# Low parts of three integer weights on GpSimd in place of VectorE, with new order tables for head and tail

## The reference

```python
xn = _layernorm(x, axis=-1)
s = _L0_attn_ref(xn, Wq, Wk, Wv, Wo)          # causal softmax attention, 16 heads of 16
g = _silu(_L0_ffn_ref(xn, w_gate, w_up, w_down))   # 256 -> 768 -> 256, weights int32 in -127..127, times 1/127
x = x + s * g
```

## Time and profile before

| | us |
|---|---|
| runs shown | 977.41, 979.42, 975.25; median 977.41 |
| profiled execution | 978.36, its span 976.6 |
| TensorE busy | 933.3 (96% of the span) |
| VectorE, ACT, GpSimd busy | 702.8, 579.5, 496.9 |

### The profile page before, as it was taken

The page is one execution under the profiler, slowest core; times in us unless marked ns, Lnnn a source line. Parts: engine busy times, 40 slices in busy tenths (PEclk is TensorE's granted clock), DMA queues, the critical chain, the costliest instruction groups (busy, mean ns, idle before and its releaser), DMA issues.

```text
span 976.6 us, 22669 instructions
## 1 busy us (share of the span) xinstructions
PE 933.3 (96%) x9034; PEld 690.7 (71%) x9034; DVE 702.8 (72%) x946; ACT 579.5 (59%) x793; POOL 496.9 (51%) x673
## 2 busy tenths in 40 slices
PE   5679999999999999999999999999999999999995
...
GB/s 259 161 68 99 133 84 141 147 132 158 122 173 96 195 126 131 158 121 171 100 183 137 132 158 122 170 99 195 126 132 157 122 173 99 192 126 132 113 101 83
DMA packets 86059, 135.01 MB, mean 138 GB/s; under 512 B 13504, under 2 KB 36288, under 8 KB 85952
## 3 DMA queue, kind: packets, MB, share of 16 engines
...
## 4 chain that ended last, share of the span: by engine, by line
PE 79%; issue 5%; DVE 4%; DMA 4%; ACT 3%; POOL 3%; SPq 1%; POOLq 0%; ACTq 0%; DVEq 0%
PE bank L191 42%; PE values L521 12%; PE bank L426 12%; PE bank L488 8%; PE bank L439 5%; ACT probs L496 2%; POOL o_compact L562 2%; DVE gated L371 1%; ACT o_hi L569 1%; SPq L314 1%; DMA o_reciprocals<-scratch_r 1%; DVE row_max L451 1%; DMA scratch_r<-sum_reciprocals 1%; PE bank L457 1%; DMA mean_and_rstd<-scratch_m 1%
## 5 line engine op out<-in xcount | busy, mean ns | idle before, releaser
L451 DVE TENSOR_REDUCE row_max<-bank 128x2 f32<-128x768 f32 (+3 forms) x352 | 384.6, 1124 | 70.2 <-PE bank L439 65.8
L496 ACT ACTIVATE probs<-bank 128x1024 f32<-128x1024 f32 x320 | 320.1, 1025 | 125.1 <-PE bank L488 125.0
L503 POOL TENSOR_SCALAR_AFFINE_SELECT probs<-probs 128x256 f32<-128x256 f32 (+1 forms) x448 | 195.3, 453 | 288.9 <-ACT probs L496 286.5
L426 PE MATMUL bank<-k_stack,q_stack 64*128 64x128 f32 (+3 forms) x1024 | 160.3, 372 | 10.7 <-DMA q_stack<-qk_hi 5.1
L521 PE MATMUL values<-probs,v 128*17 128x512 f32 (+3 forms) x2048 | 166.4, 436 | 1.8 <-POOL probs L503 1.6
L385 POOL TENSOR_TENSOR h_lo<-gated,h_hi 128x512 fp32r<-128x512 f32 x96 | 124.1, 1294 | 55.7 <-ACT h_hi L382 53.5
L488 PE MATMUL bank<-q_stack,k_stack 64*128 64x512 f32 (+3 forms) x1024 | 142.7, 351 | 6.0 <-issue 5.0
L426 PEld LDWEIGHTS bank<-k_stack,q_stack 64*128 64x128 f32 x1024 | 86.2, 189 | 79.4 <-issue 37.3
L488 PEld LDWEIGHTS bank<-q_stack,k_stack 64*128 64x128 f32 x1024 | 83.2, 186 | 46.7 <-issue 23.4
L358 DVE SCALAR_TENSOR_TENSOR gated<-gated,bank 128x512 f32<-128x512 f32 x96 | 65.7, 686 | 51.5 <-ACT gated L355 51.5
L439 PE MATMUL bank<-causal_mask,half_identities_bf 64*128 64x128 bf16 (+3 forms) x1408 | 100.4, 228 | 0.0
...
## 6 DMA issues: line engine op xcount, KB each, us to landing
...
x_in<-x SPq DMA_DIRECT2D x16, 512.0 KB, 3.7
...
x_again<-x SPq DMA_DIRECT2D x16, 512.0 KB, 4.6
...
```

What stands on the lines that cost most here:

```text
L426: nc.tensor.matmul(PS[:, n, j * keys:(j + 1) * keys], r(QS[par][low:low + STACK, pair, i * P:(i + 1) * P]), r(KS[par][low:low + STACK, pai ...
L451: signal(e.tensor_reduce(rows, scores, axis=AX.X, op=ALU.max), "d_sm")
L496: signal(e.activation(PR[:, (SCORES * beta + k) % SLOTS, :, :], both(banks), ACT.Exp, scale=SCALE_S), "d_ex")
L503: last = e.affine_select(out=diag, in_=diag, compare_op=ALU.is_ge, fill=0.0, base=0, pattern=[[0, many], [1, P]], channel_multiplier=-1)
```

## The change

GpSimd gets a new unit, `wi k`, that subtracts the high part of the k-th integer weight, with a semaphore of its own; VectorE keeps the subtraction for q, k, v and o alone. Users of g, u and d wait for the new semaphore. The cast and the high part stay in `wt`.

```diff
         def weights_split(e, beta, w):
 
             if beta == 0:
-                wait(e, c_wl, ORDER.index(w) + 1)
+                wait(e, *((c_wi, "gud".index(w) + 1) if w in "gud" else (c_wl, "kqvo".index(w) + 1)))
...
-            elif en == "dve":
-                if src.dtype == FP32:
-                    e.wait_ge(s_w[w], 16)
+            elif en == "dve" and src.dtype == FP32:
+                e.wait_ge(s_w[w], 16)
                 e.wait_ge(c_wh, k + 1)
                 e.tensor_tensor(r(W[w][1][:]).rearrange("p t n -> p (t n)"), stage,
                                 W[w][0][:].rearrange("p t n -> p (t n)"), ALU.subtract).then_inc(c_wl, 1)
...
+        def u_wi(en, e, beta, par, k, banks, prev):
+            w, src, stage = WEIGHTS[(2, 3, 6)[k]]
+            if en == "pool":
+                e.wait_ge(c_wf, k + 1)
+                e.wait_ge(c_wh, (2, 3, 6)[k] + 1)
+                e.tensor_tensor(r(W[w][1][:]).rearrange("p t n -> p (t n)"), stage,
+                                W[w][0][:].rearrange("p t n -> p (t n)"), ALU.subtract).then_inc(c_wi, 1)
...
             if en == "dve" and k == 0:
-                e.wait_ge(c_wl, len(W))
+                e.wait_ge(c_wi, 3)
```

`HEAD` and `TAIL` are new as a whole; `PERIOD` is as before. The beginning of `HEAD`, before and after:

```diff
-    ld 1 0, la 0 0, lb 0 0, wt 0 0, tr 0 0 6, tr 0 1 1, wt 0 1, wt 0 2, qk 0 0 6, wt 0 3, qk 0 1 2, wt 0 4, gg 0 0 1, wt 0 5,
-    ls 0 0, gg 0 1 5, gu 0 0 6, ls 0 1, wt 0 6, qk 0 2 2, qk 0 3 5, sm 0 0 34, mk 0 0 34, ls 0 2, sm 0 1 01, mk 0 1 01,
-    gu 0 1 6, la 1 0, hs 0 0, sm 0 2 56, xr 0 0, mk 0 2 56, sm 0 3 23, mk 0 3 23, gg 0 2 4, lm 1 0, v 0 0 1, sm 0 4 56,
...
+    la 0 0, lb 0 0, wt 0 0, ld 1 0, wt 0 1, tr 0 0 0, tr 0 1 1, wt 0 2, wt 0 3, wt 0 4, qk 0 0 6, wi 0 0, lt 1 0, qk 0 1 3,
+    la 1 0, v 0 0 6, wi 0 1, qk 0 2 0, ls 0 0, gg 0 0 6, gg 0 1 2, wt 0 5, gg 0 2 1, qk 0 3 6, gu 0 0 2, sm 0 0 01,
+    mk 0 0 01, wt 0 6, ls 0 1, sm 0 1 56, wi 0 2, lb 1 0, mk 0 1 56, sm 0 2 34, mk 0 2 34, gu 0 1 0, sm 0 3 56, mk 0 3 56,
...
```

In `TAIL` the scores come somewhat earlier, `mt 1 1` now stands ahead of `or 0 1` (before: behind it), `gg 1 3` went from behind `dn 1 0` to behind `st 1 12`, and `gu 1 3` from behind `st 1 12` to behind `gg 1 5`. A part of it, not aligned line by line:

```diff
-    sm 1 20 56, mk 1 20 56, pv 1 2, hs 1 2, sm 1 21 01, mk 1 21 01, st 1 7 45, or 0 1, pv 1 3, mt 1 1 6, st 1 8 01,
-    st 1 9 23, dn 1 0 4, gg 1 3 2, ob 0 1, st 1 10 56, pv 1 4, on 0 1, pv 1 5, st 1 11 34, od 1 0, os 0 1, st 1 12 01,
...
+    hs 1 2, pv 1 1, sm 1 21 34, od 0 1, mk 1 21 34, pv 1 2, st 1 7 01, mt 1 1 4, st 1 8 56, st 1 9 23, or 0 1, dn 1 0 0,
+    pv 1 3, st 1 10 34, ob 0 1, st 1 11 56, pv 1 4, pv 1 5, on 0 1, st 1 12 12, gg 1 3 5, os 0 1, st 1 13 23, st 1 14 01,
```

More of the change, by code:

```diff
@@ L54 @@
 HEAD = table("""
-    ld 1 0, la 0 0, lb 0 0, wt 0 0, tr 0 0 6, tr 0 1 1, wt 0 1, wt 0 2, qk 0 0 6, wt 0 3, qk 0 1 2, wt 0 4, gg 0 0 1, wt 0 5,
-    ls 0 0, gg 0 1 5, gu 0 0 6, ls 0 1, wt 0 6, qk 0 2 2, qk 0 3 5, sm 0 0 34, mk 0 0 34, ls 0 2, sm 0 1 01, mk 0 1 01,
-    gu 0 1 6, la 1 0, hs 0 0, sm 0 2 56, xr 0 0, mk 0 2 56, sm 0 3 23, mk 0 3 23, gg 0 2 4, lm 1 0, v 0 0 1, sm 0 4 56,
-    mk 0 4 56, sm 0 5 23, mk 0 5 23, sm 0 6 01, sm 0 7 56, mk 0 6 01, mk 0 7 56, sm 0 8 34, sm 0 9 01, mk 0 8 34, mk 0 9 01,
@@ new lines @@
+    la 1 0, v 0 0 6, wi 0 1, qk 0 2 0, ls 0 0, gg 0 0 6, gg 0 1 2, wt 0 5, gg 0 2 1, qk 0 3 6, gu 0 0 2, sm 0 0 01,
+    mk 0 0 01, wt 0 6, ls 0 1, sm 0 1 56, wi 0 2, lb 1 0, mk 0 1 56, sm 0 2 34, mk 0 2 34, gu 0 1 0, sm 0 3 56, mk 0 3 56,
+    sm 0 4 34, sm 0 5 12, mk 0 4 34, mk 0 5 12, sm 0 6 56, mk 0 6 56, sm 0 7 34, hs 0 0, sm 0 8 12, mk 0 7 34, hs 0 1,
+    mk 0 8 12, sm 0 9 45, mk 0 9 45, lm 1 0, sm 0 10 01, mk 0 10 01, ls 0 2, v 0 1 6, lc 1 0, fl 0 0, sm 0 11 12, ls 0 3,
+    mk 0 11 12, gu 0 2 0, mt 0 0 5, gg 0 3 6, sm 0 12 12, mk 0 12 12, sm 0 13 45, ld 2 0, mk 0 13 45, sm 0 14 23, mk 0 14 23,
@@ new lines @@
+    sm 0 15 01, mk 0 15 01, gg 0 4 6, st 0 0 23, st 0 1 45, hs 0 2, sm 0 16 01, fl 0 1, mk 0 16 01, if 0 0, st 0 2 23,
+    st 0 3 56, pv 0 0, la 2 0, sm 0 17 12, mk 0 17 12, st 0 4 34, gu 0 3 0, st 0 5 56, sm 0 18 34, mk 0 18 34, pv 0 1,
+    gg 0 5 1, gu 0 4 0, lx 1 0, gu 0 5 4, pv 0 2, st 0 6 56, sm 0 19 23, mk 0 19 23, dn 0 0 1, hs 0 3, qk 1 0 4, sm 0 20 23,
+    lm 2 0, ls 1 0, st 0 7 56, mk 0 20 23, pv 0 3, sm 0 21 01, st 0 8 45, mk 0 21 01, qk 1 1 6, gg 1 0 4, hs 0 4, ls 1 1,
+    mt 0 1 1, gu 1 0 3, gg 1 1 6, v 1 0 4, qk 1 2 3, gu 1 1 5, qk 1 3 0, st 0 9 12, sm 1 0 34, sm 1 1 56, mk 1 0 34,
@@ new lines @@
+    mk 1 1 56, st 0 10 12, pv 0 4, hs 0 5, pv 0 5, st 0 11 01, sm 1 2 34, ls 1 2, mk 1 2 34, lt 2 0, sm 1 3 56, mk 1 3 56,
+    gg 1 2 2, sm 1 4 34, mk 1 4 34, od 0 0, st 0 12 01, st 0 13 56, ls 1 3, st 0 14 01, sm 1 5 34, lc 2 0, mk 1 5 34, pv 0 6,
+    sm 1 6 56, mk 1 6 56, st 0 15 34, sm 1 7 01, mk 1 7 01, gu 1 2 2, sm 1 8 34, sm 1 9 56, or 0 0, ob 0 0, mk 1 8 34,
+    mk 1 9 56, dn 0 1 1, sm 1 10 23, st 0 16 56, mk 1 10 23, v 1 1 0, sm 1 11 45, hs 1 0, mk 1 11 45, mt 1 0 2, pv 0 7,
+    hs 1 1, st 0 17 01, on 0 0, sm 1 12 45, st 0 18 23, mk 1 12 45, pv 0 8, gg 1 3 0, sm 1 13 12, st 0 19 34, mk 1 13 12,
@@ new lines @@
+    pv 0 9, hs 1 2, st 1 0 56, pv 0 10, sm 1 14 23, mk 1 14 23, st 1 1 56, sm 1 15 01, mk 1 15 01, gu 1 3 4, pv 0 11,
+    sm 1 16 01, lb 2 0, st 1 2 23, mk 1 16 01, os 0 0, gg 1 4 4, dn 1 0 5, st 1 3 12, gu 1 4 4, sm 1 17 56, mk 1 17 56,
+    sm 1 18 23, od 0 1, zr 0 0, st 1 4 01, mk 1 18 23, gg 1 5 4, gu 1 5 6, sm 1 19 01, sm 1 20 23, lx 2 0, mk 1 19 01,
+    st 1 5 45, xr 0 0, mk 1 20 23, pv 1 0, hs 1 3, hs 1 4, pv 1 1, qk 2 0 6, pv 1 2, sm 1 21 45, ls 2 0, mk 1 21 45,
+    st 1 6 01, qk 2 1 2, mt 1 1 5, v 2 0 0, ls 2 1, gg 2 0 4, or 0 1, st 1 7 56, st 1 8 01, hs 1 5, qk 2 2 3, pv 1 3,
@@ new lines @@
+    st 1 9 45, st 1 10 12, qk 2 3 0, st 1 11 45, pv 1 4, sm 2 0 23, mk 2 0 23, sm 2 1 01, ob 0 1, st 1 12 56, mk 2 1 01,
+    on 0 1, pv 1 5, gu 2 0 4, st 1 13 23, od 1 0, ls 2 2, sm 2 2 01, mk 2 2 01, sm 2 3 56, pv 1 6, mk 2 3 56, sm 2 4 01,
+    mk 2 4 01, st 1 14 23, pv 1 7, sm 2 5 56, os 0 1, sm 2 6 12, sm 2 7 34, ls 2 3, mk 2 5 56, mk 2 6 12, mk 2 7 34,
+    dn 1 1 0, hs 2 0, op 0 0 5, sm 2 8 12, or 1 0, st 1 15 34, mk 2 8 12, gg 2 1 6, op 0 1 0, sm 2 9 34, st 1 16 56,
+    mk 2 9 34, sm 2 10 12, pv 1 8, mk 2 10 12, st 1 17 56, gu 2 1 0, mt 2 0 1, gg 2 2 4, sm 2 11 23, hs 2 1, mk 2 11 23,
@@ L84 @@
+    sm 2 12 56, st 1 18 01, mk 2 12 56, v 2 1 4, st 1 19 01, xr 1 0, sm 2 13 23, mk 2 13 23, sm 2 14 56, mk 2 14 56, pv 1 9,
+    sm 2 15 01, st 2 0 34, mk 2 15 01, pv 1 10""")
 PERIOD = table("""
```

14 lines of the change are left out of this document (7 added, 7 removed).

## The result

| | before | after |
|---|---|---|
| median of the runs beside each other, us (7 each) | 976.83 | 982.15 |
| profiled execution, us | 978.36 | 982.43 |
| its span, us | 976.6 | 980.6 |

The ratio is 1.0063, 95% interval 1.0044 to 1.0081: 5.3 us slower by the medians and 6.1 by the ratio, where +2.6 was forecast. The time lies inside the range given (975.0 to 984.5). By the ratio it lies just outside "within 0.5%", on the side to which the prediction leaned.

What follows compares the result with a forecast made beforehand. The time TensorE leaves the flag's branch was taken as the head's cost, with the middle saturated by TensorE. Head +2.3, afterwards -0.5, tail +0.8 gave +2.6 on the median 977.4: 980.0 us, range 975.0 to 984.5.

Steps and rivals of the forecast that it cites:

- Subtractions worth nothing by themselves: Head: VectorE loses 5.84 us ahead of its bound stretch, gaining nothing; GpSimd takes 3.8 us for each subtraction.
- x_in at 27.7, k stack at 31.2, u_lo at 34.5: Head landings and end, in us; the earlier x_transposed load delays the k stack by 1.5, from 29.74.
- The order on ACT: Head: third qk copy ahead of the gates' tanh; `qk 0 3` starts at 33.1, TensorE idles 6.6 us, before 5.1.
- First maximum at 38.95: Head: VectorE's first row maximum starts at 38.95 us, against 33.52 before.
- VectorE's stretch to the flag, 25.2 us: Head, first maximum to flag: 24.5 us after removing earlier work, plus 0.7 added; flag at 64.2 against 61.92.
- -0.5 afterwards: After the branch: TensorE's 0.5 us wait for xt_lo should go, -0.5 us (0 to -1.0).
- The tail, +0.8: Tail: maxima writes issued before the reciprocals make `od 1 0` 0.8 us later (0 to 1.5).
- Nothing else: Other reorderings in and behind the head: nothing, -0.5 to +0.5 us; no new TensorE waits between branch and PERIOD.
- +2.3: Head: TensorE returns from the branch at 69.1 us, 2.3 us late (bounds 0.8 to 3.9).
- (a): Rival, head: VectorE's work counts as a whole, 5.84 us come off the flag, 971.6 us; chance 0.10.
- (b): Rival, head and tail: load hidden, k stack at 29.7, tail 0; 977.7 us; chance 0.15.
- (c): Rival, head: GpSimd is the gate, TensorE waits for u_lo ending after 35.8; 981.8 to 983.1 us; chance 0.20.

Runs made afterwards that it cites:

- engine_alone: The kernel before, in its own order, with only the three subtractions moved from VectorE to GpSimd; ratio to before 1.0014.
- gates_first: The changed kernel with batch 1's power and the third qk copy moved behind gates 0 to 2 on ACT; ratio to before 1.0023.
- changed_again: The changed kernel itself, unaltered, run a second time; ratio to before 1.0060.
- values_early: The changed kernel with the second half of v moved to the gap before the scores, on a free bank; ratio to before 1.0050.
- tail_alone: The kernel before with only the new tail table; ratio to before 1.0028.
- tables_alone: The kernel before with both new order tables, VectorE still doing all the subtractions; ratio to before 1.0091.

## Why the prediction was right where it was, and wrong where it was not

The sign and the main mechanism were right; the size was less than half of what came. By its own steps:

- **Subtractions worth nothing by themselves.** Right: engine_alone. Each took 3.5 us, not 3.8, so the estimate from h_lo's 1.29 was high by 9%. Longer operations of GpSimd do not quite hold that rate: the 128x1024 one on x_transposed took 2.42 us in the kernel before, not 2.58. The 3.3 us estimated from the Trainium skill's GPSIMD Engine Reference, section Elementwise, was nearer. The advice of that page of the Trainium skill, VectorE for elementwise work, made no difference that engine_alone could show (1.0014, 0.9994 to 1.0034).
- **x_in at 27.7, k stack at 31.2, u_lo at 34.5.** 27.97, 31.32, 34.50 in the first profile; the others have 26.6 to 26.8 and 30.0 to 30.2. The load's 1.5 us is 1.4.
- **The order on ACT.** Right as the wait that ended last, and in the main term: `qk 0 3` starts at 33.38 (33.1), the gap is 6.7 us (6.6), the clock behind it 0.50. gates_first gives most of it back, but moves the waits for x_in and u_lo with it, so ACT's own share is read, not shown.
- **First maximum at 38.95.** 39.76, 38.66 and 37.48; mean 38.6. The sum has a slip: from 33.1 its own rows, 2.94 and 2.62 us, give 36.0 and 38.7 for the ends of `qk 0 3` and `gu 0 0`, not 35.8 and 38.0. Measured were 36.08 and 38.72 in the first profile, whose maximum came at 39.76. That the mean lies so near 38.95 is in part luck.
- **VectorE's stretch to the flag, 25.2 us.** This is the term that was mis-sized: 26.65, 26.6 and 26.3, so 1.3 us more. I took out old work and counted 0.7 us for what came in. VectorE's work was as counted (24.6 us of the 26.65); what was too small is its waiting, 1.8 to 2.1 us for gates. Both orders have the same four units on TensorE beside the reductions, but before, gate 3 was the third, with v behind it, and the granted clock was back at 1.00 when it began; in the new order v comes first and gate 3 is the fourth, at 0.50 (the windows above) when it begins. The rows, of before and then of after:

```profile
53.68 0.39 PE L191 MATMUL bank<-xt_hi,wg_hi 128*128 128x256 f32 x1
```

```profile
57.98 0.56 PE L191 MATMUL bank<-xt_hi,wg_hi 128*128 128x256 f32 x1
```

  In changed_again the wait fell one gate later (1.81 us), where the granted clock was 0.50 again. values_early took 0.9 of the waits away, and the stretch was 0.8 shorter. The prediction had called TensorE half fed beside VectorE; the earlier trace rows has it busy for 16.93 of 20 us, so there was little room.
- **Flag to return, 4.9 us.** 4.7, 5.1, 4.9.
- **-0.5 afterwards.** Not seen. The wait for xt_lo is gone as said, but from the return to the fifth reciprocal the three take 160.9, 161.3 and 161.6 us, and the three with the old head (before, engine_alone, tail_alone) 161.1, 161.5 and 161.2. The windows behind the branch, of before and then of after, name a candidate: the clock is full from about 70.6 in before, 3.7 us after the return, and from about 76.1 in after, 5.0 us after it. A matmul of 256 columns takes 0.21 us at the lower level and 0.12 at the upper (up 2, and the end of gate 3, in the changed kernel), so 1.3 us longer at the lower one costs about 0.6 us (an estimate from these rows), near the gain that is missing. This is read from one execution each, and not tested.

```profile
69.00:70.00 1.00, 1.00 (x6) 0.95 (x5) 0.24 (x1) 0.00 (x0) 0.64 (x2) 0.50 0.00 0
70.00:71.00 1.00, 1.00 (x12) 0.76 (x10) 0.69 (x1) 0.00 (x0) 0.00 (x0) 0.72 0.06 16
71.00:72.00 1.00, 1.00 (x14) 0.13 (x8) 0.83 (x1) 0.94 (x1) 0.00 (x0) 1.00 0.00 0
```

```profile
75.50:77.50 2.00, 2.00 (x16) 1.51 (x12) 1.09 (x2) 1.03 (x1) 0.94 (x2) 0.84 0.04 8
```

- **The tail, +0.8.** The order is as foreseen. From the tail's first issue to `od 1 0` the three with the new tail (after, changed_again, tail_alone) take 35.2 us each and those with the old one 34.8: +0.4, half of what I said. Whether it reaches the end is open (0 to +2.7, above).
- **Nothing else.** This one did not hold in full. The head came out close to its +2.3: the means of three stand 2.5 us apart at the flag (65.2 against 62.6), 2.6 at the return and 2.6 at the fifth reciprocal (231.4 against 228.7). Like with like, the three kernels with the new head have a mean ratio of 1.0063 and the three with the old one of 1.0014, which is 4.8 us, and the spans of their profiles 980.1 against 976.0, which is 4.1. Of these 4.1 us 2.6 are the head, 0.1 the tail and 1.4 lie between the fifth reciprocal and the tail's first issue, in an unchanged order. Over all fourteen executions that part is 678.1 us with the new head (nine) and 677.1 with the old (five), while repetitions of one kernel differ by 0.5 to 1.1. So 1.0 to 1.4 us may lie there, and 0.7 have no place that a trace shows. Against the kernel before alone the loss is 5.9 to 6.4 us, as engine_alone and tail_alone were themselves slower than it by 1.4 and 2.7; whether that is scatter or a cost stays open. gates_first fits in: its fifth reciprocal comes 1.6 us ahead of the old heads' mean, and its unchanged part, 679.2 us, is the longest of all, 2.2 above their mean. Why the unchanged part should be longer stays open.

Of the rivals, (a) is refuted: the first maximum is late and VectorE's 5.84 us bring nothing. (b) gave 29.7 for the stack and 977.7 for the time; the stack came at 31.32, 30.01 and 30.20 and the time was 982.15. That the load is not hidden rests on the distance from x_in's landing to the stack's, 3.3 to 3.4 us with the load ahead and 2.0 to 2.1 without, in every profile that shows both. (c) needed u_lo to end after 35.8; it ended at 34.50 and TensorE never waited for it, and in tables_alone it was out of the way and the first maximum as late. The time that (c) gave, 981.8 to 983.1, was reached, but not by its mechanism.
